# Moving the scaling and adding of attention sums from GpSimd to VectorE

## The reference, cut to what matters

```
seq = (x @ W_seq).reshape(N, 16, 32)
scores = leaky_relu(score1[:, :, None] + score2[:, None, :], 0.2)   # per head
attn = softmax(scores + (1 - adj) * -65500)
hidden = einsum('hij,jhd->ihd', attn, seq).reshape(N, 512)
x = layernorm(x + elu(hidden @ W_out + b_out))
```

## Time and profile before

| what | value |
|---|---|
| median of the timed runs | 851.83 us (851.17 to 853.32) |
| the profiled execution | 855.83 us |
| span of that execution in the trace | 853.9 us |
| mean granted TensorE clock | 0.968 |
| TensorE matmul busy | 765.0 us (90%) |
| VectorE busy | 664.9 us (78%) |
| ScalarE busy | 479.0 us (56%) |
| GpSimd busy | 168.8 us (20%) |

### The profile page before, as it was taken

One profiled execution on the slowest core, in us unless ns is written; L12 is line 12 of the kernel. 1 busy time (PEld: TensorE's weight loads), 2 busy tenths in 40 slices (PEclk: granted clock), 3 DMA queues, 4 the chain that ended last, 5 costly groups with the idle time before them and its releaser, 6 DMA issues.

```text
span 853.9 us, 24026 instructions
## 1 busy us (share of the span) xinstructions
PE 765.0 (90%) x10017; PEld 565.9 (66%) x10017; DVE 664.9 (78%) x995; ACT 479.0 (56%) x473; POOL 168.8 (20%) x159
## 2 busy tenths in 40 slices
PE   1999944989999999999999999798879999999996
PEld 0666634989999999999999999343324444444442
DVE  5677856999899999999999996789966666344444
ACT  2465626988788888998888885366431111100000
POOL 1000002233333322333333213044300000000000
PEclk9999986998999999999999999899969999999999
DMA  6566544111011111101111120421434454001110
GB/s 235 180 210 226 184 143 178 52 53 51 5 51 51 52 51 52 52 12 43 51 51 52 51 64 28 112 62 49 115 82 133 138 156 113 1 37 38 45 43 37
DMA packets 46466, 71.30 MB, mean 83 GB/s; under 512 B 1952, under 2 KB 34720, under 8 KB 42144
## 3 DMA queue, kind: packets, MB, share of 16 engines
q1 hardware_dynamic: 46384, 70.03, 24.6%
HBM read 61.37 MB, written 8.65 MB: 82 GB/s over the span
## 4 chain that ended last, share of the span: by engine, by line
issue 39%; PE 39%; DVE 12%; POOL 4%; ACT 3%; DMA 1%; DVEq 1%; POOLq 0%; SPq 0%; ACTq 0%
PE bank L577 18%; PE bank L580 10%; PE bank L502 7%; DVE RZ L997 5%; DVE RG L1008 3%; POOL RZ L469 2%; ACT RZ L747 2%; DVE RG L1012 2%; PE bank L521 2%; PE bank L509 2%; POOL rstd L465 1%; PE bank L494 1%; DMA AV<-in_L_gnn_a_dram 1%; DVE W L883 1%; DVE WA L885 1%
## 5 line engine op out<-in xcount | busy, mean ns | idle before, releaser
L577 PE MATMUL bank<-RP,RG 128*128 128x132 f16 x4096 | 372.1, 220 | 46.0 <-DVE RG L1008 23.9
L577 PEld LDWEIGHTS bank<-RP,RG 128*128 128x128 fp8e4 x4096 | 369.3, 98 | 47.9 <-issue 47.9
L580 PE MATMUL bank<-RP,MT 128*128 128x66 f16 x4096 | 371.7, 194 | 0.0
L580 PEld LDWEIGHTS bank<-RP,MT 128*128 128x128 fp8e4 x4096 | 368.3, 96 | 0.0
L747 ACT ACTIVATE RZ<-RZ,KB 128x2048 int8<-128x2048 f32 x160 | 307.1, 2024 | 0.3 <-DVE RG L1008 0.3
L1008 DVE TENSOR_TENSOR RG<-RZ,MT 128x512 int32<-128x512 int32 x160 | 136.9, 856 | 0.5 <-ACT RZ L747 0.5
L997 DVE TENSOR_SCALAR RZ<-RZ,KB 128x2048 int8<-128x2048 f32 x96 | 135.3, 1410 | 0.3 <-DVE DSL L1050 0.3
L654 PE MATMUL bank<-RG,RP 128*128 128x512 f16 x512 | 116.6, 388 | 8.7 <-DVE RG L1144 7.3
L654 PE MATMUL bank<-RZ,MT 128*128 128x512 f16 x512 | 110.7, 379 | 0.0
L654 PEld LDWEIGHTS bank<-RG,RP 128*128 128x128 bf16 x512 | 49.8, 99 | 75.6 <-DVE RG L1144 11.3
L654 PEld LDWEIGHTS bank<-RZ,MT 128*128 128x128 fp8e4 x512 | 50.1, 98 | 60.4
(11 more groups left out here) (117 smaller groups left out, 724.1 us busy)
## 6 DMA issues: line engine op xcount, KB each, us to landing
RG<-in_adj_dram SPq DMA_DIRECT2D x16, 1024.0 KB, 4.9
RZ<-s_rows_dram SPq DMA_DIRECT2D x16, 1024.0 KB, 4.7
RP<-in_adj_dram SPq DMA_DIRECT2D x16, 1024.0 KB, 5.8
RZ<-in_x_dram SPq DMA_DIRECT2D x32, 256.0 KB, 2.6
seq_copy_dram<-SEQ SPq DMA_DIRECT2D x1, 4224.0 KB, 17.3
out_dram<-W SPq DMA_DIRECT2D x16, 256.0 KB, 2.0
RZ<-in_L_gnn_W_seq_dram SPq DMA_DIRECT2D x1, 1024.0 KB, 5.2
RZ<-in_L_gnn_W_out_dram SPq DMA_DIRECT2D x1, 1024.0 KB, 5.3
```

The source lines that it names most:

```text
L577: mm(pb[bank][:, c:c + 4 * DV], G8[:, s, i * P:(i + 1) * P], PN[:, u, j, 0:4, :].rearrange("p c d -> p (c d)"), start=(j == 0 and i % IB = ...
L580: last = mm(pb[bank][:, c + 2 * DV:c + 4 * DV], MT8[:, j, i * P:(i + 1) * P], PN[:, u, j, 4:6, :].rearrange("p c d -> p (c d)"), start=Fal ...
```

## The change

`combine` goes from GpSimd's program to VectorE's, with the same three instructions on the same tiles. GpSimd keeps `prep` and the rest. In VectorE's `att_head` it is called after tile j = 13, just ahead of `hidden_head`. The wait for `hid_done` falls away, since both are now on one engine. The count of VectorE's own steps in the loop over pairs of heads goes from 6 to 10. For the last head the same three instructions stay where they were, now called through the function.

```diff
--- before.py
+++ after.py
@@ -425,35 +425,16 @@
                     w = tab[:, DS(h, 1), :].rearrange("p o t -> p (o t)").unsqueeze(2).broadcast_to([P, NT, DV])
                     gp.tensor_tensor(V2[:, :, e, :], seq_h, w, ALU.mult).then_inc(v2_ready, 1)
 
-            def combine(h, first=False):
-
-                gp.wait_ge(bank_free, h * NB + 2 * NB)
-                for e, tab in enumerate((AA, BBT)):
-                    w = tab[:, DS(h, 1), :].rearrange("p o t -> p (o t)").unsqueeze(2).broadcast_to([P, NT, DV])
-                    own.mark(gp.tensor_tensor(T[:, :, e, :], T[:, :, e, :], w, ALU.mult))
-                own.wait(gp)
-                if not first:
-                    gp.wait_ge(hid_done, h)
-                gp.tensor_tensor(ND[:, :, :], T[:, :, 0, :], T[:, :, 1, :], ALU.add).then_inc(comb_ready, 1)
-
             gp.wait_ge(tabs_done, 1)
             prep(0, 0, True)
             prep(1, 1, True)
             prep(2, 0)
-            combine(0, True)
-
             gp.wait_ge(deg_done, 1)
             gp.tensor_tensor(DINV[:, :], DINV[:, :], mhalf[:, :], ALU.pow).then_inc(pow_done, 1)
-            own_per = 4
             with gp.Fori(1, H // 2 - 1) as p:
-                own.enter(p, 1, own_per)
                 for u in range(2):
                     prep(p * 2 + (u + 1), 1 - u)
-                    combine(p * 2 + (u - 1))
-                own.leave(H // 2 - 1)
             prep(H - 1, 1)
-            combine(H - 3)
-            combine(H - 2)
             gp.wait_ge(spread_done, 1)
             own.mark(gp.partition_all_reduce(WID[:, 3:4], WID[:, 2:3], P, RMAX))
             own.wait(gp)
@@ -979,6 +960,15 @@
                     ve.wait_ge(lo_out, h * NB + (b + 1))
                     V.tensor_tensor(T[:, b * IB:b * IB + n, :, :], sums(b, n)[:, :, :, 0, :], T[:, b * IB:b * IB + n, :, :],
                                     ALU.add).then_inc(bank_free, 1)
+
+            def combine(h):
+
+                ve.wait_ge(bank_free, h * NB + 2 * NB)
+                for e, tab in enumerate((AA, BBT)):
+                    w = tab[:, DS(h, 1), :].rearrange("p o t -> p (o t)").unsqueeze(2).broadcast_to([P, NT, DV])
+                    own.mark(V.tensor_tensor(T[:, :, e, :], T[:, :, e, :], w, ALU.mult))
+                own.wait(ve)
+                V.tensor_tensor(ND[:, :, :], T[:, :, 0, :], T[:, :, 1, :], ALU.add).then_inc(comb_ready, 1)
 
             def hidden_head(h):
 
@@ -1015,6 +1005,7 @@
                     if j == AT_LOW and not last:
                         low_operands(h + 1, 1 - u)
                     if j == AT_HID and not first:
+                        combine(h - 1)
                         hidden_head(h - 1)
 
             ve.wait_ge(adjb_done, NT)
@@ -1050,7 +1041,7 @@
             V.tensor_scalar(DSL[:, :], DINV[:, :], 0.5 / XS * ZS, None, ALU.mult).then_inc(dscale, 1)
             ve.wait_ge(dscale, 3)
             with ve.Fori(1, H // 2 - 1) as p:
-                own.enter(p, 1, 6)
+                own.enter(p, 1, 10)
                 for u in range(2):
                     att_head(p * 2 + u, u)
                 own.leave(H // 2 - 1)
@@ -1058,12 +1049,7 @@
             att_head(H - 1, 1, last=True)
             high_sums(H - 1)
 
-            ve.wait_ge(bank_free, H * NB + NB)
-            ve.wait_ge(comb_ready, H - 1)
-            for e, tab in enumerate((AA, BBT)):
-                own.mark(V.tensor_tensor(T[:, :, e, :], T[:, :, e, :], tab[:, H - 1, :].unsqueeze(2).broadcast_to([P, NT, DV]), ALU.mult))
-            own.wait(ve)
-            V.tensor_tensor(ND[:, :, :], T[:, :, 0, :], T[:, :, 1, :], ALU.add).then_inc(comb_ready, 1)
+            combine(H - 1)
             hidden_head(H - 1)
 
             def general_scores():
```

## The result

The changed kernel takes 867.28 us, the median of 4 runs (865.06 to 867.90), against 851.50 us before (now the median of 4 runs): slower, with a ratio of 1.0177 and a 95% interval of 1.0153 to 1.0201. The forecast was 866.8 us. The profiled execution of the changed kernel took 865.06 us, with a span of 863.2 us.

What follows compares the result with a forecast made beforehand. VectorE's full queue, 24.36 us a head, was taken to bound the kernel, TensorE close behind at 23.90. Two-head loop 6.9 plus clock falls 8.1 made 15.0 us, on the 851.8 us median 866.8 us; range 855 to 880.

Steps and rivals of the forecast that it cites:

- The ledger of VectorE: VectorE's work per head: 24.36 us, less 3.28 of GpSimd contention, plus 2.11 for combine, 23.19 us (23.6 with prep).
- the relief: VectorE between S (banks freed) and tile 10: up to 3.28 us a head without GpSimd contention, of which only 0.98 count.
- The feed: VectorE can't do tile 10 before ScalarE's Z, 8.37 us after TensorE's last matmul of a head starts; 18.11 us follow.
- the loop: Two heads through TensorE's end, ScalarE's Z and VectorE's queue: 49.78 us against 48.72, costing 6.9 us over thirteen heads.
- The alternation: Heads alternate between 23.9 and 25.9 us, with TensorE idle 2.88 us in front of heads 4, 6, 8, 10, 12, 14.
- The clock: TensorE's clock falls after long idle times: three of six possible falls, 2.70 us each, costing 8.1 us.
- The nearest row: TensorE's closest idle time in the earlier profile, suggesting all six idle times bring a clock fall, 16.2 us.
- The bridge to the median: Adding 15.0 us to the profiled execution's 855.8 gives 870.8 us; to the median of 851.8, 866.8 us.
- TensorE's minimum, faster: Rival: VectorE isn't held at j = 10, heads take TensorE's 23.90 us, a gain of 6.0 us to 845.8; chance 0.11.
- `prep` in VectorE's way: Rival: GpSimd's L426 delays VectorE's L997 and L1008 just before S; 28.4 us slower, 880.2 us; chance 0.12.
- The signs: Expected in the profile: VectorE waiting for L747, short L1008 and L997, 2.11 us combine, TensorE's bank waits 30 us and more.

Runs made afterwards that it cites:

- e4_nomul: Changed kernel with combine's two multiplications per head each replaced by a one-column memset, the addition kept: 849.67 us, ratio 0.9978 to the kernel before.
- e5_gpbusy: Changed kernel, with GpSimd also doing instructions of combine's shape on scratch tiles where combine was: 882.94 us, ratio 1.0360 to the kernel before.
- e1: Changed kernel with combine on VectorE moved from behind tile 13 to behind tile 6: 845.49 us, ratio 0.9925 to the kernel before.
- e8: Changed kernel with combine on VectorE behind tile 11 instead of 13: 867.06 us, ratio 1.0189 to the kernel before.
- e9: Changed kernel with combine on VectorE behind tile 9 instead of 13: 844.67 us, ratio 0.9935 to the kernel before.
- e7: Kernel of e3_fill with combine's addition done twice at tile 13: 871.38 us, ratio 1.0222 to the kernel before.
- e2: Changed kernel with ScalarE's high_operands behind the Z of j = 10 instead of 8, VectorE's low_operands behind tile 11 instead of 10: 869.16 us, ratio 1.0205.
- e3_fill: Changed kernel with 16 extra unread matmuls on TensorE at the start of heads 2 to 15: 858.84 us, ratio 1.0093 to the kernel before.

## Why the prediction was right, step by step

**The ledger of VectorE.** Added 2.11 us, measured 2.10 (382.11 to 384.21). Removed up to 3.28 us less up to 0.4 for `prep`, so 2.9 to 3.3: here the size was off. The queue from S to tile 10 came out not at 5.08 us but at 5.70 where no Z holds it (e4_nomul: S at 312.09, tile 9 at 317.19, and 0.60 for it), and at 6.01 in the head shown, which also meets the Z of j = 7 and j = 8 by 0.3 us. So `combine` on GpSimd had cost VectorE 2.7 us, and `prep` keeps 0.6: L1002 lasts 1.26 us. It changed nothing in the sum, which counts only 0.98 us of the relief. The cause was right: with GpSimd busy again e5_gpbusy shows 8.33.

**The feed.** E to j = 10: 8.29 against 8.37 worked out; VectorE starts 0.03 us behind the end of the Z, not the 0.11 of the earlier trace rows. j = 10 to S: 18.11 against 18.11. Pair without a fall: 49.70 (S of head 4 at 241.50, of head 6 at 291.20) against 49.78. The threshold at j = 10 (e1, e8, e9), the half price (e4, the pairs of e7) and the second gate at j = 11 (e2) all follow from it. The 6.9 us for the loop stand against about 7.6 (e3_fill).

**The alternation.** From head 7 on E to S is 0.60 and 2.47 us in turn and the heads take 25.5 and 25.8 us with the falls in them; worked out were 0.60 and 2.58. Up to head 6 it was milder, 1.3 and 1.8 us: in this execution head 3 didn't start at TensorE's minimum. The prediction took over head 3's start from the trace of before, where a fall in head 2 had made it; in the changed kernel's profiled execution that fall came in head 1. The full alternation came only behind the fall in head 6, and with it idle times of 2.77 us in front of heads 8, 10, 12 and 14. In e3_fill, which has no fall there, the pair of 49.7 us is shared as 25.0 and 24.7 us and in the end as 24.9 and 24.8. So the loop fixes the pair, and how the two heads share it depends on how the first ones come out, which the prediction took from another execution. In the profiled execution of e8_slot11 a fall in head 2 did start it, as the prediction had assumed.

**The clock: right in sum by luck, wrong in both factors.** Three falls of 2.70 us were forecast, 8.1 us; e3_fill shows about 8. In the trace there are five falls from head 6 on (6, 8, 10, 12 and 14), and each makes a head of 24.36 us (394.21 to 418.57) from one of 22.80, so 1.56 us, 7.8 us in all. The 2.70 us came from the one fall in the trace of before: head 2, which took 25.50 us behind an idle time of 3.17, at a mean clock of 0.89; here it is 0.93. That fall was longer: the granted clock is 0.50 in the whole stretch from 192.70 to 198.60 of before, and here it is 0.50 for 3.4 us, from 395.20 to 398.60, and 1.00 behind that. The nearest row, which spoke for a fall in all six heads, would have been the better guide to the number, and the duration was the mis-sized term. An idle time of 2.09 us (before head 4) kept the clock and one of 2.06 us (before head 6) lost it, so for gaps of that size the count can't be had from their length; all four of 2.77 us and more brought a fall.

**The bridge to the median.** The spans differ by 9.3 us (863.2 - 853.9), the medians by 15.8. The profiled execution of before had its fall in head 2 and lies 4.3 us above its median; of 13 executions of that kernel on the chip of e1_slot6, the 10 at a mean clock of 0.972 took 850.4 to 851.8 us, the 3 at 0.968 took 853.0 to 855.6. The prediction added to the median what it had worked out from the profile. On the profiled execution's own time it had 870.8 us, and 865.06 was measured, 5.7 us less. On the median it was lucky: the changed kernel's other timed executions have a lower clock (0.958), so presumably more falls, than its profiled one (0.962, 865.06 us).

**The rivals.** TensorE's minimum, faster, 845.8 us: wrong for this kernel, and right to 0.3 us for the same change with combine at tile 6. What spoke for it, the cheaper instruction on VectorE (0.71 us against 1.53 and 1.98), was there; it was the place that let no gain through. `prep` in VectorE's way: in the changed kernel it didn't happen. VectorE's L987 of 391.92 and L998 of 393.11 kept their 1.28 and 0.68 us, and GpSimd's L426 beside them took 2.7 us, where two had taken 2.14:

```profile
392.01 2.73 POOL L426 TENSOR_TENSOR RP<-SEQ,TAB 128x528 f32 x1
```

Ahead of head 2 of e7_fillplus and of e5_gpbusy it did: the sign matrix took 2.11 and 2.12 us and the G behind it 1.57 in both. In the changed kernel and in the earlier trace rows VectorE's sign matrix had begun 0.09 us before the L426 and kept its 1.28 us; which of the two engines goes on later, while both still have work, these traces don't settle.

**The signs.** VectorE's waits for L747 (now L728), the short L998 and L987 and the 2.10 us of combine were as described. TensorE's waits for the banks, forecast at 30 us and more, were 27.1, since the gaps of heads 2 to 6 were smaller.

## What to carry to other kernels

Before work is moved onto an engine, find in its queue the places where another engine's result is a gate: work added ahead of a gate that it reaches early is free, the same work behind it costs. Look also for loops that close only over two rounds: they can show as alternating lengths, and a microsecond added to every round then makes each round only half a microsecond longer. Here the change as made costs 1.8%, and the same change with `combine` at tile 6 or 9 gains 0.7% over the kernel before.

## What was not expected of the hardware

TensorE's clock made idle time expensive: sixteen useless matmuls a head made the kernel 8 us faster, by filling 0.9 us of the idle time in front of a head. A fall cost 1.56 us in most heads, and up to 2.70 where it lasted longer (head 2 of before; 25.3 to 25.4 us instead of 22.8 in four heads of e5_gpbusy). In heads 1 to 15 of the traces falls came behind idle times from 1.94 us on (head 1 of the changed kernel; 7.01 before head 2 of e5_gpbusy), while one of 2.59 us (before head 2 of e1_slot6) and one of 2.65 us (before head 14 of e8_slot11) had none. Five other gaps of 2.64 to 2.66 us in that same trace had one, so the length of the gap doesn't settle it.
